# Score tiles 0 to 3 and part of attention times V as pairs of 64-row matmuls

## The reference, cut to what matters

```python
B, C1, C2, N = (8, 512, 512, 1024)
D = C2 // 8                                                  # 64
q = jnp.einsum('bcn,dc->bnd', x1, Wq) + bq
k = jnp.einsum('bcn,dc->bdn', x2, Wk) + bk[:, None]
v = jnp.einsum('bcn,dc->bdn', x2, Wv) + bv[:, None]
attn = jax.nn.softmax(jnp.einsum('bnd,bdm->bnm', q, k), axis=2)
attn_out = jnp.einsum('bcm,bnm->bcn', v, attn)
return attn_out + x1
```

## Time and profile before

| | us |
|---|---|
| median of 3 runs | 655.35 (655.29 to 655.69) |
| the profiled execution | 655.36 |
| its span, first to last instruction | 653.6 |
| outside the span | 1.8 |
| TensorE busy | 648.1 (99%) |
| VectorE busy | 466.4 (71%) |
| ScalarE busy | 290.4 (44%) |
| GpSimd busy | 115.2 (18%) |

### The profile page before, as it was taken

How to read it: one execution, slowest core, us unless ns; L and a number is a source line. 1 busy time by engine, 2 the same in 40 slices (tenths; PEclk the granted TensorE clock), 3 DMA queues, 4 the chain that set the end, 5 groups by cost and what they waited for, 6 DMA issues and landing times.

```text
span 653.6 us, 8287 instructions
## 1 busy us (share of the span) xinstructions
PE 648.1 (99%) x2852; PEld 533.3 (82%) x2852; DVE 466.4 (71%) x516; ACT 290.4 (44%) x383; POOL 115.2 (18%) x50
## 2 busy tenths in 40 slices
PE   9999999999999999999999999999999999999997
PEld 6778888888888888888888888888888888888886
DVE  5887867867768677696686966869658687587541
ACT  5886433644336433374323652345613546236120
POOL 0022200431005400063000630006300153002000
PEclk9999999999999999999999999999999999999999
DMA  8903525962249632677317763187532864325352
GB/s 309 349 1 79 149 80 145 310 172 88 90 119 312 166 107 69 154 280 177 96 64 180 268 162 96 67 211 257 139 114 76 234 231 115 128 80 129 81 163 79
DMA packets 94254, 100.10 MB, mean 153 GB/s; under 512 B 7328, under 2 KB 69024, under 8 KB 94240
## 3 DMA queue, kind: packets, MB, share of 16 engines
q1 hardware_dynamic: 94240, 99.91, 51.1%
HBM read 51.64 MB, written 16.78 MB: 105 GB/s over the span
## 4 chain that ended last, share of the span: by engine, by line
PE 98%; DVE 1%; ACT 0%; issue 0%
PE acc_ps L901 53%; PE acc_ps L870 23%; PE s_ps L840 8%; PE s_ps L848 4%; PE s_ps L849 4%; PE acc_ps L984 1%; PE acc_ps L999 1%; PE s_ps L977 1%; PE s_ps L1016 1%; PE s_ps L1009 1%; DVE pt_lo L557 1%; PE acc_ps L990 0%; DVE negmax L623 0%; DVE blocks L640 0%; ACT blocks L398 0%; PE acc_ps L971 0%
## 5 line engine op out<-in xcount | busy, mean ns | idle before, releaser
L901 PE MATMUL acc_ps<-pt_hi,vt_hi 128*128 128x512 f32 x512 | 199.4, 389 | 0.0
L901 PE MATMUL acc_ps<-pt_hi,vt_lo 128*128 128x512 f32 x512 | 199.2, 389 | 0.0
L901 PE MATMUL acc_ps<-pt_lo,vt_hi 128*128 128x512 f32 x512 | 199.2, 389 | 0.0
L410 ACT ACTIVATE probs<-s_ps,negmax 128x1024 f32<-128x1024 f32 x56 | 62.5, 1117 | 118.0 <-DVE negmax L623 118.0
L901 PEld LDWEIGHTS acc_ps<-pt_hi,vt_hi 128*128 128x128 f32 x512 | 96.1, 188 | 20.5 <-DVE vt_lo L557 0.4
L901 PEld LDWEIGHTS acc_ps<-pt_hi,vt_lo 128*128 128x128 f32 x512 | 96.1, 188 | 20.0
L901 PEld LDWEIGHTS acc_ps<-pt_lo,vt_hi 128*128 128x128 f32 x512 | 96.1, 188 | 19.9
L300 POOL TENSOR_TENSOR pt_lo<-pt_raw,pt_hi 128x1024 fp32r<-128x1024 f32 x14 | 41.0, 2950 | 360.9 <-ACT pt_hi L337 360.9
L300 POOL TENSOR_TENSOR xs_lo<-stage,xs_hi 128x1024 fp32r<-128x1024 f32 x29 | 72.0, 2484 | 114.4 <-ACT xs_hi L337 113.9
L870 PE MATMUL acc_ps<-wv_hi,xs_hi 128*128 128x512 f32 x224 | 87.1, 389 | 0.0
L870 PE MATMUL acc_ps<-wv_lo,xs_hi 128*128 128x512 f32 x224 | 87.1, 389 | 0.0
(11 more groups left out here) (89 smaller groups left out, 680.3 us busy)
## 6 DMA issues: line engine op xcount, KB each, us to landing
pt_raw<-blocks SPq DMA_DIRECT2D x240, 128.0 KB, 2.4
stage<-in_x_dram SPq DMA_DIRECT2D x32, 512.0 KB, 6.7
o_sb<-in_x_dram SPq DMA_DIRECT2D x64, 256.0 KB, 3.3
out_dram<-o_sb SPq DMA_DIRECT2D x64, 256.0 KB, 2.5
stage<-in_ctx_dram SPq DMA_DIRECT2D x31, 512.0 KB, 8.9
pt_raw<-in_L_xattn_Wv_dram SPq DMA_DIRECT2D x4, 256.0 KB, 6.9
stage<-in_ctx_dram SPq DMA_DIRECT2D x2, 256.0 KB, 3.6
pt_raw<-in_L_xattn_Wk_dram SPq DMA_DIRECT2D x1, 128.0 KB, 4.4
```

The source lines that it names most:

```text
L410: nc.scalar.activation(probs[:, t % 2, :], s_ps[:, t % 2, :, :].rearrange("p a n -> p (a n)"), ACT.Exp, bias=negmax[:, t:t + 1], accum_out ...
L901: mm = nc.tensor.matmul(acc_ps[:, c % BANKS, :], v[:, m, cols], p[:, m, :], start=(m == 0 and v is vt_hi and p is pt_hi), stop=(m == MT - ...
```

## The change

For the seven batches that follow another, score tiles 0 to 3 are made by `scores_rows`: six matmuls of 64 rows instead of four of 128. They come in three pairs; one of a pair uses partitions 0 to 63 and writes the first half of the columns, the other uses partitions 64 to 127 and writes the second half. The pairs are high x high, low x high and high x low; low x low is left out. For this both parts of q must lie in both halves of the partitions: `q_dup` is `q_st` (first 512 positions) with its halves exchanged, made by two copies on ACT (`q_second`).

The steps (2, 3) to (2, 7) and (3, 0) to (3, 4) of h = 1, which stand between these tiles, are made by `out_rows`: each of their three matmuls becomes a pair of 64-row matmuls, whose upper one writes bank c and whose lower one writes bank c - 2. DVE then needs two instructions for c = 2 and c = 3: the one of before on bank c - 2, and an addition of bank c that waits for it. As more banks are busy at the end, the V groups use the banks in another order (`V_BANK`) and wait for other counts (`V_FREE`). The prologue, the last batch's own steps and score tiles 4 to 7 are as they were.

```diff
+V_BANK = (0, 2, 1, 3, 0, 2, 1, 3)
+V_FREE = (3, 3, 4, 4, 5, 6, 7, 8)
+ROWS_FROM = {2: 3, 3: 0}
+ROWS_TO = {2: MT, 3: 5}
...
+            def q_second(b):
+
+                act.wait_ge(s_qhi, b * 2)
+                copy(q_dup[D:2 * D, :], q_st[0:D, 0:NH].bitcast(F32)).then_inc(s_qdup_hi, 1)
+                act.wait_ge(s_qlo, b * 2)
+                copy(q_dup[0:D, :], q_st[D:2 * D, 0:NH].bitcast(F32)).then_inc(s_qdup_lo, 1)
...
                     round_x2(nb, 3)
+                    q_second(nb)
                 for j in range(PAIRS):
                     p_hi(b, 1, j)
...
+            def out_rows(b, c):
+
+                dve.wait_ge(s_o, b * OG + CT + c + 1)
+                dve.wait_ge(s_res[c], half_of(b, 1) * 16 + 16)
+                nc.vector.scalar_tensor_tensor(
+                    out=o_sb[:, c, :], in0=acc_ps[:, c - 2, :], scalar=bias_v[:, c:c + 1],
+                    in1=o_sb[:, c, :], op0=ALU.add, op1=ALU.add).then_inc(s_side, 1)
+                dve.wait_ge(s_side, b * 2 + c - 1)
+                nc.vector.tensor_tensor(o_sb[:, c, :], acc_ps[:, c, :], o_sb[:, c, :], ALU.add).then_inc(s_acc, 1)
...
                 turn(nb, 0)
-                out(b, 1, 2)
+                out_rows(b, 2)
                 normalise(nb, 1)
...
                 turn(nb, 2)
-                out(b, 1, 3)
+                out_rows(b, 3)
                 normalise(nb, 3)
...
+            def scores_rows(t):
+
+                rows = slice(t * P, (t + 1) * P)
+                for q_top, q_low, k in ((q_st, q_dup, k_hh), (q_dup, q_st, k_hh), (q_st, q_dup, k_ll)):
+                    nc.tensor.matmul(s_ps[:, t % 2, 0, :], q_top[0:D, rows], k[0:D, 0:NH],
+                                     start=(q_top is q_st and k is k_hh), stop=(k is k_ll))
+                    mm = nc.tensor.matmul(s_ps[:, t % 2, 1, :], q_low[D:2 * D, rows], k[D:2 * D, NH:N],
+                                          start=(q_top is q_st and k is k_hh), stop=(k is k_ll))
+                mm.then_inc(s_s, 1)
...
                 if t == 0:
                     pe.wait_ge(s_qsum, b + 1)
                     pe.wait_ge(s_qlo, b * 2 + 1)
+                    pe.wait_ge(s_qdup_hi, b)
+                    pe.wait_ge(s_qdup_lo, b)
                     pe.wait_ge(s_klo, b * 2 + 2)
...
-                scores(t)
+                scores_rows(t)
...
-                    pe.wait_ge(s_acc, b * ACC + m + 1)
+                    pe.wait_ge(s_acc, b * ACC + V_FREE[m])
...
+            def out_rows(b, c, m):
+
+                if m == 0:
+                    pe.wait_ge(s_acc, b * ACC + MT + CT + c + 1)
+                if m == ROWS_FROM[c]:
+                    pe.wait_ge(s_acc, b * ACC + BANKS + MT + CT + c - 1)
+                cols = slice(c * P, (c + 1) * P)
+                for v, p in ((vt_hi, pt_hi), (vt_hi, pt_lo), (vt_lo, pt_hi)):
+                    nc.tensor.matmul(acc_ps[:, c, :], v[0:D, m, cols], p[0:D, m, :],
+                                     start=(m == 0 and v is vt_hi and p is pt_hi),
+                                     stop=(m == MT - 1 and v is vt_lo))
+                    mm = nc.tensor.matmul(acc_ps[:, c - 2, :], v[D:2 * D, m, cols], p[D:2 * D, m, :],
+                                          start=(m == ROWS_FROM[c] and v is vt_hi and p is pt_hi),
+                                          stop=(m == ROWS_TO[c] - 1 and v is vt_lo))
...
-                        out_part(b, 1, c, m)
+                        if not last and c in ROWS_FROM and ROWS_FROM[c] <= m < ROWS_TO[c]:
+                            out_rows(b, c, m)
+                        else:
+                            out_part(b, 1, c, m)
```

More of the change, by code:

```diff
@@ L85, in build @@
         q_st = sb("q_st", [P, N], F32R)
+        q_dup = sb("q_dup", [P, NH], F32R)
         k_hh = sb("k_hh", [P, N], F32R)
@@ L158, in build @@
         s_qlo = sem("s_qlo")
+        s_qdup_hi = sem("s_qdup_hi")
+        s_qdup_lo = sem("s_qdup_lo")
+        s_side = sem("s_side")
         s_khi = sem("s_khi")
@@ L419, in v_hi @@
                 act.wait_ge(s_v, b * MT + m + 1)
-                copy(vt_hi[:, m, :], acc_ps[:, m % BANKS, :]).then_inc(s_vhi, 1)
+                copy(vt_hi[:, m, :], acc_ps[:, V_BANK[m], :]).then_inc(s_vhi, 1)
             def p_hi(b, h, j):
@@ L662, in v_lo @@
                 dve.wait_ge(s_vhi, b * MT + m + 1)
-                sub(vt_lo[:, m, :], acc_ps[:, m % BANKS, :], vt_hi[:, m, :]).then_inc(s_acc, 1)
+                sub(vt_lo[:, m, :], acc_ps[:, V_BANK[m], :], vt_hi[:, m, :]).then_inc(s_acc, 1)
             def p_lo(b, h, j):
@@ L859, in scores_first, with scores_next_rows @@
                     pe.wait_ge(s_ksum, b + 1)
-                scores(t)
+                scores_rows(t)
+            def scores_next_rows(b, t):
+                pe.wait_ge(s_exp, b * ST + t - 1)
+                scores_rows(t)
             def scores_next(b, t):
@@ L869, in v_tile @@
                 for x, w in ((xs_hi, wv_hi), (xs_hi, wv_lo), (xs_lo, wv_hi)):
-                    mm = nc.tensor.matmul(acc_ps[:, m % BANKS, :], x[:, k, cols], w[:, k, :],
+                    mm = nc.tensor.matmul(acc_ps[:, V_BANK[m], :], x[:, k, cols], w[:, k, :],
                                           start=(k == 0 and w is wv_hi and x is xs_hi),
@@ L903, in out_part @@
                                           stop=(m == MT - 1 and v is vt_lo))
+                if m == MT - 1:
+                    mm.then_inc(s_o, 1)
+                elif c == CT - 1 and m % 2:
+                    mm.then_inc(s_used, 1)
+            def out_rows(b, c, m):
[11 more added lines that the diff above has]
+                                          stop=(m == ROWS_TO[c] - 1 and v is vt_lo))
                 if m == MT - 1:
@@ L953, in batch @@
                             if (c, m) == (3, 1):
-                                scores_next(nb, 2)
+                                scores_next_rows(nb, 2)
                             if (c, m) == (3, 5):
-                                scores_next(nb, 3)
-                        out_part(b, 1, c, m)
+                                scores_next_rows(nb, 3)
+                        if not last and c in ROWS_FROM and ROWS_FROM[c] <= m < ROWS_TO[c]:
+                            out_rows(b, c, m)
+                        else:
+                            out_part(b, 1, c, m)
                 if last:
```

## The result

| | before | changed |
|---|---|---|
| median | 655.32 us (655.15 to 655.69, 4 runs) | 660.2 us (658.98 to 660.5, 4 runs) |
| ratio, 95% interval | | 1.007 (1.0053 to 1.0088) |
| the profiled execution | 655.36 | 658.98 |
| its span | 653.6 | 657.2 |

The account below looks back on a forecast made before the run. TensorE, 99% busy, bounds the kernel, with a loop through VectorE and SP's transfers only 1.28 us behind; two additions of 1.38 us overrun it: 6 x 0.27 + 1.38 = 3.0 us on 655.36 gives 658.3 us, range 652.0 to 667.0.

Parts of the forecast that it names:

- The likeliest case: VectorE's additions delay the path to v_lo 7, TensorE waits at m = 7 each batch: 658.3 us, chance 0.57.
- rival A: TensorE's path decides, faster: additions fall into pauses, each batch saves 0.37 us, 652.8 us; chance 0.14.
- A pair costs one slot: On TensorE, two 64-row matmuls with their two weight loads take one matmul slot, 0.227 us.
- rival B: TensorE's pairs cost more than a slot: 659.7 to 719 us; chance 0.12 mildly (to 668), 0.09 heavily.
- the rival drawn from it: TensorE's pairs bear the loss of four 32-row tiles, 1.30 slots each: about 673 us.
- Layout changes: TensorE going to pairs and back, twice a batch: 0.27 us each, 0.54 us for two.
- Second addition: On VectorE, ahead of the turn of tile 3: 0.69 us each, 1.38 us for two a batch.
- Nothing else on this path moves: Start of VectorE's path, new waits, V group 2 and ACT's two copies: counted 0, nothing charged.
- 0.27 us a batch: At TensorE's step m = 7: v_lo 7 0.10 us late plus 0.17 us of restart, in six batches.
- TensorE's saving: TensorE alone reaches m = 7 about 0.37 us earlier; this only lengthens its wait there.
- The third batch, 1.38 us: The batch whose margin at m = 7 was already used: the additions' whole 1.38 us counts.
- The sum: Whole kernel: 6 x 0.27 + 1.38 = 3.0 us added to 655.36 us, giving 658.3 us.

Follow-up runs that it names:

- e1: Kernel before plus only a second VectorE addition behind the last two outs of a batch (bank c added twice), no pairs: 659.45 us, ratio 1.006.
- e2: Changed kernel without the second addition, so bank c of the last two groups is left out of the output: 652.16 us, ratio 0.9953.
- e10: e4 with all eight steps of c = 2 and c = 3 as pairs, 18 pairs more a batch: 655.75 us, ratio 0.9999.
- e3: Changed kernel with the ten steps between score tiles as whole matmuls again, no second addition, eight layout changes a batch: 660.88 us, ratio 1.0087.
- e6: Changed kernel with the out of c = 3 and its addition behind the turn of tile 3, its store behind the 16 transfers: 654.15 us, ratio 0.9983.
- e4: Changed kernel with v_lo 7 moved ahead of neg_max 7 and the turn of tile 6: 653.37 us, ratio 0.9972.
- e8: Changed kernel run once more, unedited, for a second profile: 658.62 us, ratio 1.0053 against the kernel before.
- e9: Changed kernel with bank c - 2 copied by ACT and added by GpSimd instead of VectorE, c = 3 stored behind the transfers: 664.59 us, ratio 1.0147.
- e5: Kernel before with v_lo 7 moved ahead of neg_max 7 and the turn of tile 6, control for e4: 655.83 us, ratio 1.0007.
- e7: e6 with v_lo 7 also ahead of the maximum of tile 7: 654.14 us, ratio 0.9981.
- e11: e9 with GpSimd's two additions starting only after the turn of tile 3, both stores behind the 16 transfers: 652.51 us, ratio 0.9959.

## Why the prediction was right

The likeliest case came true: slower, by the path through VectorE, with the wait where it was expected. The median of 660.2 lies in the range and 1.9 us above the 658.3 forecast. The range, 652.0 to 667.0, is so wide that it also holds rival A's 652.8 and no change at all; what bears the mechanism out is the wait in all seven batches, e1 and e2. Step by step:

- **A pair costs one slot: right.** 0.23 us apart in the trace, 0.0006 us by e10. Two loads that pass one behind the other (rival B) would have filled the slot; the rows show them side by side. The Trainium skill, "TensorE: Matmul & The Clock Gate", section "Measured speedup vs the span model", has loss when four tiles of 32 rows run at once (3.07 times). Pairs of 64 rows show none here, so the rival drawn from it, 673 us, falls.
- **Layout changes: too dear by a tenth.** 0.54 us charged, 0.49 by e2's period and by the starts with their tail; 0.44 where the tail is cut short (e3). The term was in the right place, one part ahead of tile 0 and one behind tile 3. The Trainium skill, "TensorEngine Tiling (Array Packing)", section "Tiling Modes", says that a change of mode drains the engine, and gives no size; the later starts fit that. The saving by TensorE's own path was 0.42 us, forecast 0.37.
- **Second addition: nearly right.** 1.38 us forecast, 1.43 measured. The wait between the two instructions is as taken (0.03 us, 338.64 + 0.71 to 339.38), but the addition takes 339.99 - 339.38 = 0.61 us from start to start, not the 0.57 of `v_lo`.
- **Nothing else on this path moves: right.** The maximum of tile 0 starts as it did by the plan (1.33 us in both), 12.4 and 12.04 us stayed, and the copies on ACT, the new banks and V group 2 cost nothing in e2. With e6 the last of these showed how far: the `out` put behind the turn of tile 3 was enough to make V group 2 wait.
- **0.27 us a batch: right.** The five batches beside the third took 0.18 to 0.29 more, the last 0.36; e1 and the changed kernel have 80.06 to 80.07 for 79.79. That TensorE's saving would not enter, and only make the wait longer, is what e1 against the changed kernel shows.
- **The third batch, 1.38 us: 1.53 measured**, by luck in part. The earlier trace rows were read as a slow issue on SP, and in that trace they are: 11.95 us, then 200.18 - 186.37 - 11.95 = 1.86 us to the turn, as elsewhere. In the changed kernel the issue took 10.50 us and the landing was late, 202.38 - 188.47 - 10.50 = 3.41 us behind it; the sum is nearly the same, 13.91 us after 13.81, against 12.4 in other batches. The prediction took it over without asking whether it would come again. From the end of the turn of tile 3 to the start of that of tile 4 this batch has 13.7 to 14.0 us in both kernels and in e1, e4, e8 and e9, 13.3 in e10, 13.2 in e5 and 12.8 in e3, but 12.4 to 12.6 in e2, e6, e7 and e11. Without it the same sum would have given 7 x 0.27 = 1.9 us. What delays it is open, but one thing goes with it: each trace has nine transfers of the instruction queue (q8 on the page). In the nine traces with a late group one of them starts between the group's first issue and its last landing (at 189.0 us before, during the issue; at 199.8 in the changed kernel, behind it), and in the four others it starts only after the landing (e2: 199.2, with the landing at 198.6). This holds in all 13 traces, but no run moved that transfer alone, so it is a lead and not a cause shown.
- **The sum: 3.0 us forecast, 3.62 in the profiled execution.** The terms above make 1.25 + 0.36 + 1.53 = 3.14; the remaining 0.48 us lies ahead of the first pair. The median of the first runs says 4.9 and that of e8 3.3; the gap of 1.6 us between them is the part that neither the forecast nor the traces explain. That the forecast is only 0.6 us off in the profiled execution is helped by the third batch's luck, and the 0.48 us belong to no term of it.
- **Rival A** had the right price for TensorE's saving (2.6 us forecast; e2 saved 3.1) and the wrong path in front. With e4 and e11 it becomes true.
- What the prediction left out was the last batch, whose h = 1 has no pairs and no scores between. Its split has so little room that e1, e4, e5 and e10 wait there and lose 0.5 to 2.1 us, while the changed kernel itself does not. In e1, e5 and e10 the 16 transfers ahead of it took 11.5 to 11.9 us to issue instead of 10.5, again with a transfer of the instruction queue among them; the kernel before had 11.3 us there too and no wait, and e4 waits with 10.5.

## What to carry to other kernels

An engine at 99% can hide a loop through three others and the transfers that is nearly as long, so measure the loop and its margin before giving any of its engines more work: here 1.28 us of margin turned a saving of 0.42 us a batch on TensorE into a loss of 0.27. Once such a loop decides, the cure is anywhere on it, not where the work was added; moving one instruction ahead of two others (e4) did as much for the period as taking the additions away (79.37 us in both). Work that is moved to an idle engine can still hold up the engine it was taken from (e9), and has to be placed in time as well as in a queue (e11).

## What the runs showed of the hardware

- Two matmuls of 64 rows by 512 columns on the two halves of the array cost what one of 128 rows costs, 0.227 us, each with its own weight load.
- Going from whole matmuls to pairs costs 0.25 us, and so does going back: 0.20 us in the first two distances and 0.05 spread over some nine more. With only three pairs between the changes the two cost 0.44 us together.
- A VectorE scaling of 128 x 1024 that takes 0.75 us takes 1.85 us when a GpSimd addition of 1.29 us starts with it.
- One group of 16 transfers in seven, in the same batch, lands 1.4 us late in both kernels and in e1, e4 and e8, by a longer issue (11.95 us instead of 10.5) or by a later landing; less late in e9, e10, e5 and e3, and on time in e2, e6, e7 and e11. A loop without margin pays for this in full (1.5 us), one with 1.7 us of margin (e4) pays 0.1 us.
